# Transposed probabilities leave PSUM through VectorE instead of ScalarE, in a latent-attention transformer layer on eight cores

## The chip, the cores and the metric

The kernel runs on the 8 cores of one Trainium2 chip, one batch element per core, with the same program on each. No core talks to another. The metric is the device time in microseconds of the slowest core. In the text, PE is TensorE, DVE is VectorE, ACT is ScalarE, POOL is GpSimd and SP is the queue engine SyncE.

## The reference

The layer takes x of shape 8 x 2048 x 2048 (batch, tokens, features) in float32. It is attention with a latent bottleneck, then a gated feed-forward block, each with a residual and a layer norm behind it.

```python
q = rmsnorm(x @ q_a_w.T, q_a_ln_w) @ q_b_w.T          # 16 heads, 128 + 64 each
ckv_full = x @ kv_a_w.T                               # 512 latent + 64 rotary
kv = rmsnorm(ckv_full[..., :512], kv_a_ln_w) @ kv_b_w.T
k_nope, v = kv[..., :128], kv[..., 128:]              # per head
# rotary on q_pe and on the one k_pe that all heads share
scores = einsum('bhqd,bhkd->bhqk', query, key_s) * SCALE
probs  = softmax(where(causal, scores, -inf))
attn   = einsum('bhqk,bhkd->bhqd', probs, v)
x = layernorm(x + attn @ o_w.T)
x = layernorm(x + ffn(x))     # silu(g) * u, ternary weights with scales, 5632 wide
```

## The kernel before

The program writes the instruction stream of each engine by hand. `P.op` puts one instruction at the end of an engine's list and can increment a semaphore; `P.w` and `P.wf` put a wait there. Each engine works its list in order, so the order of the calls is the order of the work. The semaphores that matter here are `sAct` (counts ACT's results), `vE` and `vStat` (DVE's results), `tTR` (transposes done by PE) and `tMM` (other matmuls).

The stages follow each other with a barrier between (`gate`): projections of x, the queries, the attention heads (line 589 on), the output projection with the first layer norm, and the feed-forward block.

The attention stage loops over 16 heads. For each head PE forms the keys `kfm` and the values `vtm` out of the latent `c_fm`, and ACT copies them out of PSUM (lines 648 and 666). Then a loop runs over `qc`, the 16 chunks of 128 queries, with two more turns to drain it. A chunk `qc` sees (qc+1)*128 keys, in groups of up to 512 columns, so it has one group for chunks 0 to 3 and four groups for chunks 12 to 15. The scores of a group go to one of five 512-column regions of PSUM (`ring`: four in `pS`, one in `pX`). One turn `qc` does this, in the order of the code:

- For each group PE multiplies queries by keys (line 692), adds the causal mask to the last group (699) and adds the rotary part (703). DVE takes the row maximum of the group (710).
- For the chunk two turns back, `pqc` = qc-2, PE transposes the probabilities in blocks of four tiles of 128 (line 745). The transpose is a matmul of `Ebuf` with `Dg`, a diagonal matrix with the reciprocals of the row sums. The result in `pPT` (two buffers) is copied to `PTsb` (two buffers, line 752). `emit_pv` multiplies the values by it into `pO` (729), one block behind the transposes. ACT copies `pO` to `OX` (763).
- DVE forms the negated maximum over the groups (769). ACT takes the exponential of each group with it as bias, and the row sums with it (778, two instructions each: the activation and the reading of the accumulator).
- DVE adds up the row sums (785), takes the reciprocal (789) and forms `Dg` (793).

Chunk `pqc` has `nkt` = pqc+1 tiles, so its copies are one to four blocks, the last of one to four tiles. There are 40 copies a head, 640 in all. A region of the ring is free again when the exps of its group are done. `pts_free` makes a copy wait until `PTsb` has been multiplied, and `ppt_free` makes the transposes wait until `pPT` has been copied. The same list, under the name `pw_free`, guards these two PSUM buffers where the next head forms its keys.

## Time and profile before

| What | us |
|---|---|
| Median of 2 runs | 5739.92 |
| Lowest and highest of them | 5714.51, 5765.32 |
| The profiled execution, its own time | 5654.77 |
| Its span on the slowest core (core 1) | 5653.3 |
| Spans of the eight cores | 5617.7 to 5653.3 |

The span runs from the first to the last instruction of one core; the execution's own time is 1.5 us longer than it. Rows of the profile give an engine, a line of the kernel, what is written from what, and how long. A busy PE is not PE at its peak, since matmuls overlap. "Idle before" names what ended an engine's wait. Over the whole span PE is busy for 68%, DVE for 33%, ACT for 29%, POOL for 6%.

### The profile page before, as it was taken

How to read it: one execution, taken by the hardware profiler on the slowest of the kernel's cores; microseconds unless marked ns; L12 is line 12 of the kernel's file. 1: busy time of each engine (PE TensorE's matmuls, PEld its weight loads, DVE VectorE, ACT ScalarE, POOL GpSimd, SP SyncE). 2: the span in 40 equal slices, each digit the busy share in tenths (PEclk: the TensorE clock that was granted, in tenths of full speed). 3: DMA queues.
4: the chain of work that ended last, by engine and by line, in shares of the span. 5: the costliest groups of instructions: out<-in, count | busy, mean ns of one | idle time of the engine just before them, and what ended most of it. 6: DMA issues, size and time to landing. Idle time of an engine off the chain costs nothing.

```text
span 5653.3 us, 67407 instructions; the slowest of 8 cores (5617.7 to 5653.3 us)
## 1 busy us (share of the span) xinstructions
PE 3870.8 (68%) x20400; PEld 1847.0 (33%) x20400; DVE 1866.8 (33%) x3822; ACT 1635.9 (29%) x3420; POOL 331.7 (6%) x581
## 2 busy tenths in 40 slices
PE   0456556656666666666355669885998599859986
PEld 0222222223333333333122223342444244424443
DVE  2222322444333333333223233323332233223323
ACT  0000000006565656565100013322332233223322
POOL 0000000000000000000000001111111111101110
PEclk9877778888877878887577779998999899989998
DMA  4111012100000000000311049875887589758975
GB/s 128 44 30 30 27 42 60 30 26 5 9 5 9 5 10 5 9 7 3 103 62 38 30 122 265 272 241 186 282 280 250 190 276 278 243 191 276 283 250 172
DMA packets 209874, 674.49 MB, mean 119 GB/s; under 512 B 30272, under 2 KB 30784, under 8 KB 205440
## 3 DMA queue, kind: packets, MB, share of 16 engines
q1 hardware_dynamic: 130608, 359.51, 20.8%
q0 software_dynamic: 78928, 310.68, 17.1%
q8 instruction: 187, 3.06, 0.2%
q14 instruction: 151, 1.24, 0.1%
HBM read 653.05 MB, written 16.78 MB: 118 GB/s over the span
## 4 chain that ended last, share of the span: by engine, by line
PE 34%; DMA 31%; DVE 13%; issue 11%; ACT 9%; DVEq 1%; SPq 0%; ACTq 0%; POOL 0%; POOLq 0%
DMA stg_gp<-up_l 19%; PE pD L1068 6%; DMA stg_gp<-down_c 5%; PE pPT L526 5%; PE pOP L864 4%; ACT Ebuf L778 4%; PE pQA L362 3%; PE pO L729 3%; ACT PTsb L752 2%; DVE ubf L229 2%; DMA stage<-ow_l 2%; PE pPT L745 2%; DVE stats L710 2%; PE pS L692 2%; PE pPT L641 1%
## 5 line engine op out<-in xcount | busy, mean ns | idle before, releaser
L997 PE MATMUL pU<-OX,ubf 128*128 128x512 bf16 x2816 | 648.6, 384 | 127.3 <-DVE ubf L229 126.4
L988 PE MATMUL pG<-OX,gbf 128*128 128x512 bf16 x2816 | 644.1, 382 | 128.6 <-ACT gbf L226 128.6
L1068 PE MATMUL pD<-h_fm,dbf 128*128 128x512 bf16 x2816 | 636.2, 382 | 84.5 <-DVE dbf L229 80.1
L229 DVE CAST ubf<-stg_gp 128x1024 bf16<-128x1024 f32 x352 | 244.6, 695 | 868.0 <-DMA stg_gp<-up_l 849.3
L729 PE MATMUL pO<-PTsb,vtm 128*128 128x128 bf16 x2176 | 251.3, 248 | 311.8 <-ACT PTsb L752 308.5
L997 PEld LDWEIGHTS pU<-OX,ubf 128*128 128x128 bf16 x2816 | 270.5, 99 | 493.1 <-issue 195.5
L988 PEld LDWEIGHTS pG<-OX,gbf 128*128 128x128 bf16 x2816 | 276.9, 98 | 466.8 <-issue 140.1
L1068 PEld LDWEIGHTS pD<-h_fm,dbf 128*128 128x128 bf16 x2816 | 272.8, 98 | 426.4 <-issue 127.3
L1010 ACT ACTIVATE sig<-pG,gates_sb 128x512 bf16<-128x512 f32 x176 | 120.9, 687 | 872.0 <-DVE tmid L1015 612.7
L226 ACT CAST gbf<-stg_sy 128x1024 bf16<-128x1024 f32 x352 | 351.3, 1040 | 70.8 <-DMA stg_sy<-gate_l 70.5
L752 ACT CAST PTsb<-pPT 128x512 bf16<-128x512 f32 (+3 forms) x640 | 312.6, 524 | 201.3 <-PE pPT L745 200.5
L526 PE MATMUL pPT<-rmsqa_fm,qbw_bf 128*128 128x512 bf16 x1152 | 277.4, 403 | 135.4 <-DVE qbw_bf L191 135.3
L864 PE MATMUL pOP<-ow_bf,OX 128*128 128x512 bf16 x1024 | 278.0, 439 | 109.5 <-DVE ow_bf L191 106.9
L778 ACT ACTIVATE Ebuf<-pS,stats 128x512 bf16<-128x512 f32 (+3 forms) x512 | 314.3, 621 | 88.9 <-DVE stats L769 87.8
L710 DVE TENSOR_REDUCE stats<-pS 128x1 f32<-128x512 f32 (+3 forms) x512 | 289.6, 599 | 122.6 <-PE pS L703 122.0
L226 ACT CAST dbf<-stg_sy 128x1024 bf16<-128x1024 f32 (+1 forms) x192 | 174.3, 971 | 538.0 <-PE pD L1068 538.0
L229 DVE CAST dbf<-stg_gp 128x1024 bf16<-128x1024 f32 (+1 forms) x192 | 122.5, 649 | 546.5 <-DMA stg_gp<-down_c 285.0
L729 PEld LDWEIGHTS pO<-PTsb,vtm 128*128 128x128 bf16 x2176 | 156.8, 108 | 389.8 <-issue 387.9
L221 POOL DMA_DIRECT2D stg_gp<-up_l x352 | 207.4, 589 | 1225.1 <-DVE ubf L229 1113.7
L745 PE MATMUL pPT<-Dg,Ebuf 128*128 128x128 bf16 x2176 | 254.7, 255 | 26.5 <-DVE stats L710 23.5
L692 PE MATMUL pS<-kfm,Q_all 128*128 128x512 bf16 (+3 forms) x512 | 215.2, 420 | 69.1 <-ACT Ebuf L778 42.7
L362 PE MATMUL pQA<-qa_w_bf,x0fm_t 128*128 128x512 bf16 x768 | 235.8, 421 | 20.9 <-DVE x0fm_t L345 20.9
(132 smaller groups left out, 3745.6 us busy)
## 6 DMA issues: line engine op xcount, KB each, us to landing
stg_gp<-up_l POOLq DMA_DIRECT2D x352, 512.0 KB, 6.2
stg_sy<-gate_l SPq DMA_DIRECT2D x352, 512.0 KB, 6.4
stg_sy<-down_c SPq DMA_DIRECT2D x128, 512.0 KB, 5.6
stg_gp<-down_c POOLq DMA_DIRECT2D x128, 512.0 KB, 5.2
stg_sy<-down_c SPq DMA_DIRECT2D x64, 384.0 KB, 6.2
stg_gp<-down_c POOLq DMA_DIRECT2D x64, 384.0 KB, 4.4
stage<-x SPq DMA_DIRECT2D x64, 256.0 KB, 3.2
stage<-ow_l SPq DMA_DIRECT2D x64, 256.0 KB, 3.3
```

What stands on the lines that cost most here:

```text
L226: e.copy(d[:, a:a + cc], tiles[i][:, 0:cc]), inc=cP)
L229: e.tensor_copy(d[:, a:a + cc], tiles[i][:, 0:cc]), inc=cP)
L362: P.op("tensor", lambda e, i=i, d=d, j=j, st=st, sp=sp: e.matmul(pQA[:, j * 512:(j + 1) * 512], x0fm_t[i][:, d * 128:(d + 1) * 128], qa_w_ ...
L526: P.op("tensor", lambda e, pb=pb, sk=slots[k], k=k, cc=cc, piece=piece: e.matmul(pW[pb][:], qbw_bf[:, sk * 512 + cc * 128:sk * 512 + (cc + ...
L710: P.op("vector", lambda e, g=g, n=n, rt=rt, off=off, par=par: e.reduce_max(stats[:, par + g:par + g + 1], rt[:, off:off + n], axis=AX), in ...
L729: P.op("tensor", lambda e, kt=kt, bb=bb, sl=sl, nkt=nkt: e.matmul(pO[:, 0:128], vtm[:, kt * 128:(kt + 1) * 128], PTsb[sl][:, bb * 128:(bb ...
L752: P.op("scalar", lambda e, bn=bn, sl=sl: e.copy(PTsb[sl][:, 0:bn * 128], pPT[sl][:, 0:bn * 128]), inc=sAct)
L778: P.op("scalar", lambda e, ei=ei, g=g, n=n, rt=rt, off=off, par=par: e.activation(Ebuf[ei][:, g * 512:g * 512 + n], rt[:, off:off + n], AF ...
L864: P.op("tensor", lambda e, hv=hv, t=t, j=j, st=st, sp=sp: e.matmul(pOP[:, j * 512:(j + 1) * 512], OX[:, hv * S + t * 128:hv * S + (t + 1) ...
L988: P.op("tensor", lambda e, wi=wi, d=d, gc0=gc0: e.matmul(pG[wi][:], gbf[wi][:, d * 128:(d + 1) * 128], OX[:, d * S + gc0:d * S + gc0 + 512 ...
L997: P.op("tensor", lambda e, wi=wi, d=d, gc0=gc0: e.matmul(pU[wi][:], ubf[wi][:, d * 128:(d + 1) * 128], OX[:, d * S + gc0:d * S + gc0 + 512 ...
L1068: P.op("tensor", lambda e, di=di, hh=hh, jj=jj, ii=ii: e.matmul(pD[di][:], dbf[hh][:, jj * 128:(jj + 1) * 128], h_fm[:, ii * 512:(ii + 1) ...
```

## The change

The copy of the transposed probabilities out of PSUM is taken from ACT and given to DVE. The waits that go with it follow: the copy's own waits stand in DVE's list, it increments `vE` instead of `sAct`, and both PE's product with `PTsb` and the next use of `pPT` wait on `vE`.

```diff
                             def emit_pv(sl, b0, bn, ev):
                                 nonlocal first_pv
-                                P.w("tensor", sAct, ev)
+                                P.w("tensor", vE, ev)
...
-                                P.w("scalar", tTR, tTR.n)
-                                P.wf("scalar", pts_free[sl])
-                                P.op("scalar", lambda e, bn=bn, sl=sl: e.copy(
-                                    PTsb[sl][:, 0:bn * 128], pPT[sl][:, 0:bn * 128]), inc=sAct)
-                                ppt_free[sl] = (sAct, sAct.n)
+                                P.w("vector", tTR, tTR.n)
+                                P.wf("vector", pts_free[sl])
+                                P.op("vector", lambda e, bn=bn, sl=sl: e.tensor_copy(
+                                    PTsb[sl][:, 0:bn * 128], pPT[sl][:, 0:bn * 128]), inc=vE)
+                                ppt_free[sl] = (vE, vE.n)
                                 if pvq is not None:
                                     emit_pv(*pvq)
-                                pvq = (sl, b0, bn, sAct.n)
+                                pvq = (sl, b0, bn, vE.n)
```

DVE's list at the end of a head, before the change. The first rows are the maxima of chunk 15 (L710) and its negated maximum (L769), then the sum, the reciprocal and Dg of chunk 15, and the cast of the next head's weights:

```order
L710 TENSOR_REDUCE stats<-pS 128x1 x3
L710 TENSOR_REDUCE stats<-pX 128x1
L769 TENSOR_REDUCE stats<-stats 128x1
L785 TENSOR_REDUCE stats<-stats 128x1
L789 RECIPROCAL stats<-stats 128x1
L793 TENSOR_SCALAR Dg<-cI,stats 128x128
L191 CAST kvw_bf<-stage 128x512 x2
```

The same place after the change:

```order
L710 TENSOR_REDUCE stats<-pS 128x1 x3
L710 TENSOR_REDUCE stats<-pX 128x1
L752 CAST PTsb<-pPT 128x512 x3
L752 CAST PTsb<-pPT 128x256
L769 TENSOR_REDUCE stats<-stats 128x1
L785 TENSOR_REDUCE stats<-stats 128x1
L789 RECIPROCAL stats<-stats 128x1
L793 TENSOR_SCALAR Dg<-cI,stats 128x128
L752 CAST PTsb<-pPT 128x512 x3
L752 CAST PTsb<-pPT 128x384
L752 CAST PTsb<-pPT 128x512 x4
L191 CAST kvw_bf<-stage 128x512 x2
```

The copies of chunk 13 (14 tiles) stand between the maxima of chunk 15 and its negated maximum; those of chunks 14 and 15 stand behind Dg and ahead of the cast of the weights.

ACT's list at the same place before the change, with the copies of chunk 13, the output copy (L763), the exps of chunk 15 (L778) and the copies of chunks 14 and 15:

```order
L752 CAST PTsb<-pPT 128x512 x3
L752 CAST PTsb<-pPT 128x256
L763 CAST OX<-pO 128x128
L778 ACTIVATE Ebuf,stats<-pS,stats 128x512 x3
L778 ACTIVATE Ebuf,stats<-pX,stats 128x512
L752 CAST PTsb<-pPT 128x512 x3
L752 CAST PTsb<-pPT 128x384
L763 CAST OX<-pO 128x128
L752 CAST PTsb<-pPT 128x512 x4
L763 CAST OX<-pO 128x128
L648 CAST kfm<-pPT 128x512 x4
```

And after it:

```order
L763 CAST OX<-pO 128x128
L778 ACTIVATE Ebuf,stats<-pS,stats 128x512 x3
L778 ACTIVATE Ebuf,stats<-pX,stats 128x512
L763 CAST OX<-pO 128x128 x2
L648 CAST kfm<-pPT 128x512 x4
```

Every PTsb row is gone from ACT's list, and what is left there keeps its order. The lists of PE, POOL and SP have the same rows as before.

## Rows read from the trace of the kernel before

**Rows 1.** The attention stage in the view by stage: us, busy time of each engine.

```profile
1237.00:2737.00 1500.00, 999.19 (x7199) 554.76 (x7197) 545.03 (x1715) 880.14 (x2497) 1.74 (x3) 0.80 0.03 8
```

**Rows 2.** Timeline of one head: first and last negated maximum, last output copy.

```profile
2465.11 0.15 DVE L769 TENSOR_REDUCE stats<-stats 128x1 f32<-128x1 f32 x1
...
2529.66 0.16 DVE L769 TENSOR_REDUCE stats<-stats 128x1 f32<-128x4 f32 x1
...
2541.52 0.27 ACT L763 CAST OX<-pO 128x128 bf16<-128x128 f32 x1 [0.62 <-PE pO L729]
```

**Rows 3.** Timeline (start, duration, engine), one turn, chunk 13 to 14 of a head.

```profile
2427.11 0.69 ACT L778 ACTIVATE Ebuf<-pS,stats 128x512 bf16<-128x512 f32 x1
...
2427.77 0.49 ACT L778 ACTIVATE Ebuf<-pS,stats 128x256 bf16<-128x256 f32 x1
...
2428.45 0.16 DVE L785 TENSOR_REDUCE stats<-stats 128x1 f32<-128x4 f32 x1 [3.20 <-ACT Ebuf L778]
...
2428.55 0.72 PE L745 MATMUL pPT<-Dg,Ebuf 128*128 128x128 bf16 x8
...
2429.08 1.07 ACT L752 CAST PTsb<-pPT 128x512 bf16<-128x512 f32 x2 [0.73 <-PE pPT L745]
2429.22 1.28 DVE L710 TENSOR_REDUCE stats<-pS 128x1 f32<-128x512 f32 x2
...
2430.02 0.38 PE L729 MATMUL pO<-PTsb,vtm 128*128 128x128 bf16 x4 [0.75 <-ACT PTsb L752]
...
2431.01 0.55 DVE L710 TENSOR_REDUCE stats<-pS 128x1 f32<-128x384 f32 x1
...
2431.67 0.16 DVE L769 TENSOR_REDUCE stats<-stats 128x1 f32<-128x4 f32 x1
2432.14 0.27 ACT L763 CAST OX<-pO 128x128 bf16<-128x128 f32 x1 [0.51 <-PE pO L729]
...
2432.31 0.69 ACT L778 ACTIVATE Ebuf<-pS,stats 128x512 bf16<-128x512 f32 x1
```

**Rows 4.** Groups by line and form: busy us, mean ns of one, idle before.

```profile
L752 ACT CAST PTsb<-pPT 128x512 bf16<-128x512 f32 (+3 forms) x640 | 312.6, 524 | 201.3 <-PE pPT L745 200.5
...
L752 ACT CAST PTsb<-pPT 128x512 bf16<-128x512 f32 x448 | 249.1, 589 | 165.4 <-PE pPT L745 164.9
L345 DVE CAST x0fm_t<-pTR 128x512 bf16<-128x512 f32 x64 | 44.3, 692 | 57.8 <-PE pTR L339 57.8
L710 DVE TENSOR_REDUCE stats<-pS 128x1 f32<-128x512 f32 x352 | 228.3, 683 | 0.4 <-issue 0.4
L710 DVE TENSOR_REDUCE stats<-pS 128x1 f32<-128x128 f32 x48 | 13.7, 285 | 122.0 <-PE pS L703 122.0
```

**Rows 5.** Who waited for whom in the attention stage: us in total, times, longest.

```profile
DVE stats L785 <- ACT Ebuf L778: 498.3, 255, 3.9
...
PE pO L729 <- ACT PTsb L752: 308.5, 368, 3.2
```

**Rows 6.** Timeline of the output projection: a DVE copy from PSUM and PE behind it.

```profile
3013.41 0.69 DVE L846 CAST OX<-pTR 128x512 bf16<-128x512 f32 x1 [0.84 <-PE pTR L839]
3014.25 0.58 PE L839 MATMUL pTR<-cI,x1tm 128*128 128x128 bf16 x4 [0.94 <-DVE OX L846]
```

**Rows 7.** Two stretches of a head by stage (granted clock behind POOL), and transposes in the first's clock.

```profile
2484.00:2488.00 4.00, 3.13 (x19) 1.73 (x17) 1.93 (x6) 2.45 (x7) 0.00 (x0) 0.50 0.02 4
...
2505.00:2510.00 5.00, 3.60 (x28) 1.73 (x28) 2.31 (x7) 3.64 (x10) 0.00 (x0) 1.00 0.02 3
...
2476.03 0.63 PE L745 MATMUL pPT<-Dg,Ebuf 128*128 128x128 bf16 x4
```

**Rows 8.** Timeline at the end of a head, after the exps of chunk 15.

```profile
2532.80 1.09 ACT L752 CAST PTsb<-pPT 128x512 bf16<-128x512 f32 x2
...
2533.63 0.26 DVE L793 TENSOR_SCALAR Dg<-cI,stats 128x128 bf16<-128x128 bf16 x1 [0.18 <-DVE stats L789]
2533.76 0.58 PE L729 MATMUL pO<-PTsb,vtm 128*128 128x128 bf16 x4 [3.09 <-ACT PTsb L752]
```

## Prediction

> **What bounds the kernel now.** I read the stages first, then the attention stage instruction by instruction. The stage view gives the attention stage 1500 us of the 5653.3 us span, with PE busy for 999, ACT for 880 and DVE for 545 us of it [rows 1]. No engine is full, so a chain of waits sets the time there. The groups that the change moves are ACT's 640 copies of PTsb, 312.6 us in all: 448 are of 512 columns, 0.589 us each [rows 4], all in this stage. The waits of the stage look like an invitation to move them: DVE stands idle for 498.3 us behind ACT's exps, and PE waits 308.5 us for these copies [rows 5].
>
> One turn of the loop over query chunks shows who waits for whom; rows 3 are the turn from chunk 13 to chunk 14 of one head. ACT's exps of 512 columns start 0.66 us apart (2427.11 to 2427.77). When the last has ended, DVE sums (2428.45), takes the reciprocal, scales Dg and starts the maxes of the next chunk at 2429.22: 1.00 us after the last exp's own slot of 0.45 us (2427.77 + 0.45 = 2428.22). The four maxes start 0.60 us apart. The negated max stands at 2431.67, and exps can follow it by 0.25 us. Beside this, and on ACT, which is idle then, the copies of chunk 12 start at 2429.08, before the first max. PE multiplies with them from 2430.02, the output copy of OX comes at 2432.14 and the next exps at 2432.31.
>
> So before, the loop is exps, sum and Dg, maxes, negated max, exps, and the copies lie beside the maxes. I test that with a sum over one head, whose negated maxes run from 2465.11 (chunk 0) to 2529.66 (chunk 15), 64.55 us [rows 2]. Chunk q has q/4 (rounded down) full groups of 512 columns and one ragged group. That makes 21 full groups of exps (chunks 0 to 14) by 0.665 us = 14.0, 15 ragged ones by about 0.50 = 7.5, 24 full groups of maxes (chunks 1 to 15) by 0.60 = 14.4, 15 ragged by 0.41 = 6.2, and 15 stretches of 1.00 from exps to maxes = 15.0. The ragged values are means that I estimate between the rows at 512 and those at fewer columns. That is 57.1 us; with 0.43 us from the end of the last max's slot to the exps in each turn (15 by 0.43 = 6.5) it makes 63.6, against 64.55 measured. The copies thus cost at most about 1 us a head now.
>
> **The change part by part.** Every copy of PTsb goes from ACT to DVE, 640 of them; the waits of PE on them change only the semaphore. The text of PE, POOL and SP is the same. What matters is the place on DVE: behind all maxes of chunk q, ahead of the negated max of chunk q, the copies of chunk q-2 stand now. DVE works in order, so three things follow.
>
> First, the duration. A copy of this form on DVE takes 0.692 us (the same form, TensorE's output to a 16-bit tile) against 0.589 on ACT [rows 4], and PE follows it 0.84 us after its start (3013.41 to 3014.25) [rows 6]. Alone that is 0.10 us for each copy on the path.
>
> Second, the place. The copies can start only behind the last max: one slot after its start, at about 2431.5 in rows 3 (2431.01 and some 0.46 for 384 columns) instead of 2429.08, 2.4 us later. The 0.43 us at the end of the loop is replaced by a chain C: copy, product, OX copy, exps. With PE at 2.4 GHz four 128-column matmuls take 0.38 us and 0.21 of PE's time; at 1.2 GHz 0.63 and 0.43 [rows 3, 7]. From a matmul's end to OX 0.10, from OX to the exps 0.17.
> One block of four tiles: 0.84 + 0.38 + 0.26 = 1.48 us (1.73 at 1.2 GHz).
> Two blocks: the second copy starts 0.60 later: 2.08 (2.33).
> Three: the third transposes use the first's buffer, so they follow the first copy and the first product: 0.84 + 0.21 + 0.38 + 0.12 until the third copy, 0.84 for it, 0.38 + 0.26 behind it: 3.03 (0.84 + 0.43 + 0.63 + 0.12 + 0.84 + 0.63 + 0.26 = 3.75).
> Four: the fourth copy 0.60 behind the third: 3.63; at 1.2 GHz its transposes are the later ones, and it is 4.61.
> Each tile that the last block lacks takes off 0.13 for the copy (maxes of 128 and 512 columns take 0.285 and 0.683 [rows 4], and the copy at 512 takes the same as a max) and 0.05 (0.11) for each PE group of the last block on the path: one with up to two blocks and with four, two with three blocks (and with four at 1.2 GHz).
>
> Now the turns of a head. Chunks 2 to 5 copy one block, 6 to 9 two, 10 to 13 three, 14 and 15 four, and within each class the last block has 1, 2, 3, 4 tiles. The clock is 1.2 GHz (0.50) in the early turns and 2.4 (1.00) later, rising behind chunk 7 [rows 7]. The sums of C are then 5.5 + 7.3 + 10.7 + 6.3, and 0.43 for chunk 1, which copies nothing: 30.2 us. With 1.2 GHz throughout they are 5.5 + 7.9 + 12.9 + 7.6 + 0.43 = 34.3. The body of a head becomes 57.1 + 30.2 = 87.3 us (91.4), against 64.55: 22.8 us more (26.9).
>
> Third, the end of the head. The copies of chunk 14 start at 2532.80 now, straight behind ACT's exps. On DVE they come behind Dg of chunk 15, which starts at 2533.63 and is followed 0.17 later: 1.0 us later. PE already waits for them there, 3.09 us [rows 8]. These and the copies of chunk 15 form a chain with some eight links, each 0.10 us longer. Together 1.8 us. The cast of the next head's weights falls behind these copies too; it takes 0.43 us and lies beside the last product, so I count nothing (without that cover, at most 0.4 us a head, 7 in all).
>
> What is unloaded from ACT buys nothing: exps wait for OX's copy, which needs the last product, and that needs the last copy. The later stages are untouched.
>
> Sum: 22.8 + 1.8 = 24.6 us a head at the present clock, by 16 heads 394 us; with PE at 1.2 GHz throughout, 28.7 by 16 = 459 us. The turns grow by a third with the same matmuls in them, so PE is less busy, and I expect the higher clock to be lost in a part of the turns: I take the middle, 425 us. The profiled execution took 5654.77 us (its span is 5653.3), which makes 6080 us. It was 1.5% below the median of the runs shown, 5739.92, and the result will be such a median, so the forecast is 5740 + 425 = 6165, say 6160 us.
>
> DVE's pace is weighed against one page. The maxes in rows 3 start 0.60 us apart though each lasts 0.68. The Trainium skill, VectorE: DVE Perf Modes, section "The DRAIN you can't avoid", says that the next operation does not start until the pipe is empty. By that rule each further copy in a row would cost 0.08 us more, some 25 of them a head, 2 us, or 30 us in all; by the row nothing. The trace disagrees with the rule for maxes, and I go by the row.
>
> **The rivals.** *The clock stays at 1.2 GHz.* Worked out above: 459 us, 5740 + 459 = 6199. For it: PE's share of busy time falls in every turn. Against it: in the late turns the clock stays at 1.00 although PE already waits in every turn.
>
> *The copies find a hole in DVE.* If the maxes of a chunk were done before its predecessor's transposes, a copy would start when it does now, and only the 0.10 us for each link would be left: about 27 links a head by 0.10 by 16 = 43 us, 5783, no measurable difference. DVE's idle 498.3 us speaks for it; but that idle time lies ahead of the sum at 2428.45, while the copies are wanted at 2429.08, when the maxes begin. It would need maxes that start at least 2.4 us earlier.
>
> *ACT is what the loop waits for* (the other sign). If the exps stood ready and only the copies kept ACT from them, the move would free them. The place is the copies ahead of each group of exps: 312.6 us of ACT's 880. At the end of a head the copies of chunk 14 do stand behind the exps for about 2.5 us. If a quarter of those 312 us were on the path, the time would fall by 78 us to 5662. It decides in favour where the negated max is ready long before the exps start; in rows 3 it is 0.64 us earlier, and OX's copy, not PTsb's, is what comes last. The Trainium skill, TensorEngine Tiling (Array Packing), section "PSUM Bottleneck", advises to use both ScalarE and VectorE for emptying PSUM, which is this rival's rule. By it the step gains; the rows above say that DVE is in the loop exactly when it would be needed.
>
> **How the numbers follow.** My forecast (the clock lost in part) has a chance of 0.60, the clock lost throughout 0.33, the hole in DVE 0.04, ACT as the bound 0.03. The first two are both slower. A measurement of this kernel can tell about 2%, 115 us, from no change. So slower by over 2% has 0.93, within 2% 0.05 (the hole, and a small gain of the third), faster 0.02. The range: at its low end 5655 + 394 = 6049 if the new runs are like the profiled one; at its high end the slower of the runs shown, 5765, with 459 = 6224; the sum for 64.55 us fell short by 1 us a head, and the rule on DVE gives 30 us, so I allow about 45 us above and 30 below: 6020 to 6270.
>
> **What would show it right or wrong.** The attention stage grows from 1500 to about 1925 us, the other stages keep their times. PTsb's copies on DVE take 0.69 us at 512 columns. In a late turn the first copy starts one slot (0.2 to 0.6 us) behind the last max's start, and PE's wait for the copies grows from 308.5 us by several hundred. A turn with four groups takes 9.1 to 10 us instead of 6.6, one with a single group about 1 us more. ACT's busy time falls by some 310 us and its idle time grows by over 700. The granted clock of the stage falls below 0.80. I am wrong if the copies start before the maxes end, if the negated max comes later than OX's copy, or if the late turns stay under 8 us.

## The result and the profile after

The changed kernel takes 6129.99 us in the median of 11 runs, against 5742.74 us of the kernel before in the runs beside it. The ratio is 1.0776 with a 95% interval of 1.0706 to 1.0846: slower by 7.8%. (It leaves out executions in which some cores ran some per cent slower at a lower clock, whatever the kernel; both medians contain such, so they differ by less, 387 us or 6.7%.) The median lies inside the range of the forecast and 30 us below its value. The profiled execution took 6138.3 us.

The head of the profile page, PE's line and the line of the copies, of the kernel after:

```profile
span 6136.8 us, 67407 instructions; the slowest of 8 cores (6069.4 to 6136.8 us)
...
PE 4075.5 (66%) x20400; PEld 1952.4 (32%) x20400; DVE 2194.7 (36%) x4462; ACT 1318.8 (21%) x2780; POOL 328.2 (5%) x581
...
L752 DVE CAST PTsb<-pPT 128x512 bf16<-128x512 f32 (+3 forms) x640 | 368.6, 604 | 126.1 <-PE pPT L745 124.8
```

The attention stage of the kernel after, in the view by stage (us, busy time of PE, PE's weight loads, DVE, ACT and POOL, granted clock); it answers to [rows 1]:

```profile
1301.00:3259.00 1958.00, 1148.27 (x7187) 644.83 (x7185) 868.89 (x2349) 564.28 (x1857) 1.74 (x3) 0.66 0.02 7
```

The stage grew from 1500 to 1958 us. ACT's busy time fell by 316 us, DVE's rose by 324, and the granted clock fell from 0.80 to 0.66. I compare this stage between kernels by the time from the first to the last output copy (L763): 1274.9 to 2725.9 before, 1338.0 to 3248.1 after, 1451 against 1910 us, so 459 us more. Over the eight cores of the same executions it is 1445 to 1457 and 1910 to 1917 us. The whole span differs by 483.5. The rest lies in stages that the change does not touch: the first output copy came 63 us later in this one execution, while it stands between 1273 and 1289 in every run of the experiments, and the stages behind attention were 39 us shorter.

Who waits for whom in that stage of the kernel after, us in total, times, longest; it answers to [rows 5]:

```profile
ACT OX L763 <- PE pO L729: 1210.0, 256, 7.4
...
PE pO L729 <- DVE PTsb L752: 677.1, 398, 4.4
DVE stats L785 <- ACT Ebuf L778: 642.1, 256, 3.9
```

PE's wait for the copies has doubled, from 308.5 to 677.1 us, and ACT waits 1210 us for the products. DVE, now the engine with more work, waits more for the exps than before (642 against 498 us). No engine became full: a chain got longer. The turn from chunk 13 to chunk 14 of one head, timeline of the kernel after; it answers to [rows 3]:

```profile
2855.85 0.69 ACT L778 ACTIVATE Ebuf<-pS,stats 128x512 bf16<-128x512 f32 x1
...
2857.85 0.49 ACT L778 ACTIVATE Ebuf<-pS,stats 128x256 bf16<-128x256 f32 x1
...
2858.53 0.16 DVE L785 TENSOR_REDUCE stats<-stats 128x1 f32<-128x4 f32 x1 [3.60 <-ACT Ebuf L778]
...
2859.18 1.06 PE L745 MATMUL pPT<-Dg,Ebuf 128*128 128x128 bf16 x8
2859.30 1.28 DVE L710 TENSOR_REDUCE stats<-pS 128x1 f32<-128x512 f32 x2
...
2861.09 0.55 DVE L710 TENSOR_REDUCE stats<-pS 128x1 f32<-128x384 f32 x1
2861.56 1.28 DVE L752 CAST PTsb<-pPT 128x512 bf16<-128x512 f32 x2
2862.60 0.58 PE L729 MATMUL pO<-PTsb,vtm 128*128 128x128 bf16 x4 [2.35 <-DVE PTsb L752]
...
2864.59 0.15 DVE L769 TENSOR_REDUCE stats<-stats 128x1 f32<-128x4 f32 x1
...
2865.41 0.27 ACT L763 CAST OX<-pO 128x128 bf16<-128x128 f32 x1 [6.98 <-PE pO L729]
2865.57 0.69 ACT L778 ACTIVATE Ebuf<-pS,stats 128x512 bf16<-128x512 f32 x1
```

Exps to exps is 9.72 us. PE has begun the transposes at 2859.18, but the copy starts at 2861.56, right behind the last max. From there it is 4.01 us to the next exps. The negated max (2864.59) is ready 0.98 us before them.

The end of the same head: the copies of chunk 14 (2879.29) now follow Dg of chunk 15, and PE waits 4.04 us for them, where it was 3.09 [rows 8].

```profile
2879.12 0.26 DVE L793 TENSOR_SCALAR Dg<-cI,stats 128x128 bf16<-128x128 bf16 x1 [0.18 <-DVE stats L789]
2879.29 1.29 DVE L752 CAST PTsb<-pPT 128x512 bf16<-128x512 f32 x2
2880.34 0.58 PE L729 MATMUL pO<-PTsb,vtm 128*128 128x128 bf16 x4 [4.04 <-DVE PTsb L752]
```

### The profile page after: what moved, and what is told of

It is laid out like the page before. It is cut to its first block, busy times and chain, and to the rows that moved or that the text cites. A ratio compares the mean times of both kernels' runs of the same rounds, so it can differ in the third digit from the quotient of the medians.

```text
span 6136.8 us, 67407 instructions; the slowest of 8 cores (6069.4 to 6136.8 us)
## 1 busy us (share of the span) xinstructions
PE 4075.5 (66%) x20400; PEld 1952.4 (32%) x20400; DVE 2194.7 (36%) x4462; ACT 1318.8 (21%) x2780; POOL 328.2 (5%) x581
## 4 chain that ended last, share of the span: by engine, by line
PE 36%; DMA 28%; DVE 17%; issue 12%; ACT 5%; DVEq 1%; SPq 0%; POOL 0%; ACTq 0%; POOLq 0%
DMA stg_gp<-up_l 17%; PE pD L1068 5%; PE pPT L526 5%; DMA stg_gp<-down_c 5%; PE pOP L864 4%; PE pO L729 4%; PE pQA L362 4%; DVE PTsb L752 4%; DVE stats L710 3%; ACT Ebuf L778 3%; PE pPT L745 2%; PE pS L692 2%; DVE ubf L229 2%; PE pS L703 2%; DMA stage<-ow_l 2%
## 5 line engine op out<-in xcount | busy, mean ns | idle before, releaser
L729 PE MATMUL pO<-PTsb,vtm 128*128 128x128 bf16 x2176 | 294.9, 280 | 677.8 <-DVE PTsb L752 677.1
L729 PEld LDWEIGHTS pO<-PTsb,vtm 128*128 128x128 bf16 x2176 | 183.4, 121 | 767.7 <-issue 764.8
L752 DVE CAST PTsb<-pPT 128x512 bf16<-128x512 f32 (+3 forms) x640 | 368.6, 604 | 126.1 <-PE pPT L745 124.8
L526 PE MATMUL pPT<-rmsqa_fm,qbw_bf 128*128 128x512 bf16 x1152 | 295.7, 422 | 135.0 <-DVE qbw_bf L191 134.8
L710 DVE TENSOR_REDUCE stats<-pS 128x1 f32<-128x512 f32 (+3 forms) x512 | 289.6, 599 | 122.5 <-PE pS L703 122.5
L763 ACT CAST OX<-pO 128x128 bf16<-128x128 f32 x256 | 67.8, 265 | 1210.0 <-PE pO L729 1210.0
L778 ACT ACTIVATE Ebuf<-pS,stats 128x512 bf16<-128x512 f32 (+3 forms) x512 | 315.3, 625 | 40.5 <-DVE stats L769 39.6
L745 PE MATMUL pPT<-Dg,Ebuf 128*128 128x128 bf16 x2176 | 289.0, 287 | 25.3 <-DVE stats L710 25.2
L692 PE MATMUL pS<-kfm,Q_all 128*128 128x512 bf16 (+3 forms) x512 | 265.7, 519 | 23.5 <-ACT Ebuf L778 8.8
L362 PE MATMUL pQA<-qa_w_bf,x0fm_t 128*128 128x512 bf16 x768 | 263.0, 461 | 20.8 <-DVE x0fm_t L345 20.8
```

The lines of the kernel that those rows point to most:

```text
L362: P.op("tensor", lambda e, i=i, d=d, j=j, st=st, sp=sp: e.matmul(pQA[:, j * 512:(j + 1) * 512], x0fm_t[i][:, d * 128:(d + 1) * 128], qa_w_ ...
L526: P.op("tensor", lambda e, pb=pb, sk=slots[k], k=k, cc=cc, piece=piece: e.matmul(pW[pb][:], qbw_bf[:, sk * 512 + cc * 128:sk * 512 + (cc + ...
L710: P.op("vector", lambda e, g=g, n=n, rt=rt, off=off, par=par: e.reduce_max(stats[:, par + g:par + g + 1], rt[:, off:off + n], axis=AX), in ...
L729: P.op("tensor", lambda e, kt=kt, bb=bb, sl=sl, nkt=nkt: e.matmul(pO[:, 0:128], vtm[:, kt * 128:(kt + 1) * 128], PTsb[sl][:, bb * 128:(bb ...
L752: P.op("vector", lambda e, bn=bn, sl=sl: e.tensor_copy(PTsb[sl][:, 0:bn * 128], pPT[sl][:, 0:bn * 128]), inc=vE)
L778: P.op("scalar", lambda e, ei=ei, g=g, n=n, rt=rt, off=off, par=par: e.activation(Ebuf[ei][:, g * 512:g * 512 + n], rt[:, off:off + n], AF ...
```

## The experiments

The stage is the time between the first and the last output copy on the slowest core of one profiled execution; over the eight cores of one execution it spreads by 1 to 17 us, so differences of that size say nothing. The clock is that of the stage. Runs are the lowest and the second lowest time (of e3 the lowest alone); where a ratio to the kernel before (same chip) has an interval, it is given.

| Kernel | copies on | stage, us | clock | runs, us | ratio |
|---|---|---|---|---|---|
| before | ACT | 1451 | 0.80 | 5647, 5656 | 1 |
| changed | DVE | 1910 | 0.66 | 6101, 6104 | 1.0776 (1.0706 to 1.0846) |
| e1 late sums | DVE | 1640 | 0.73 | 5840, 5867 | |
| e2 late sums | ACT | 1414 | 0.80 | 5605, 5609 | |
| e3 negated max first | DVE | 2008 | 0.65 | 6202 | |
| e4 copies twice | ACT | 1802 | 0.67 | 6012, 6014 | |
| e5 filler matmuls | DVE | 1845 | 0.77 | 6008, 6013 | 1.0628 (1.0570 to 1.0686) |
| e6 alternate | both | 1627 | 0.73 | 5809, 5816 | 1.0270 (1.0234 to 1.0306) |
| e7 late sums, max last | DVE | 1527 | 0.79 | 5707, 5721 | 1.0105 (1.0067 to 1.0143) |
| e8 late sums, split, late out | both | 1361 | 0.80 | 5540, 5541 | 0.9782 (0.9745 to 0.9818) |
| e9 late sums, late out | ACT | 1340 | 0.81 | 5549, 5571 | 0.9814 (0.9744 to 0.9885) |
| e10 late sums, late out | DVE | 1512 | 0.76 | 5694, 5703 | |
| e11 maxes between copies | DVE | 1737 | 0.66 | 5930, 5946 | 1.0495 (1.0448 to 1.0541) |
| e12 copy's wait last | DVE | 1852 | 0.68 | 6052, 6061 | |

**e1: sums and Dg one turn later, behind the copies.** The statements of L784 to L795 (sum, reciprocal, Dg, and the entry in `pendq`) become a function `late_stats` that is called one turn later, behind the copies, and in the first draining turn ahead of them. The negated max goes ahead of the copies.

```diff
+                        if qc < TC:
+                            P.w("vector", vStat, vStat.n)
+                            P.op("vector", lambda e, ngr=ngr, par=par: e.reduce_max(
+                                stats[:, par + 4:par + 5], stats[:, par:par + ngr],
+                                axis=AX, negate=True), inc=vStat)
+                            neg_done = vStat.n
-                        if len(pendq) >= 2 or (qc >= TC and pendq):
+                        if pendq and pendq[0][0] <= qc - 2:
...
                             po_free = (sAct, sAct.n)
+                        if late is not None:
+                            late()
+                            late = None
...
                             exp_done = sAct.n
+                            late = late_stats
```

> The changed kernel (copies on DVE), with DVE's sum, reciprocal and Dg of chunk q-1 put behind the maxes, the negated max and the copies of turn q, where they stood ahead of the maxes of turn q. DVE then need not wait for the exps before it takes the next maxes. Theory A (the copies are dear because DVE stands in the loop exps, sum, Dg, maxes, copies, product, exps): most of the loss comes back, 20 to 31 us a head, 320 to 490 us in all, so 5640 to 5810 us. Rival B (the copy itself is dear on DVE, by its duration or by contention): the 640 copies are all still there, so the time stays within 50 us of 6130. Rival C (the clock is what costs): it comes back only as far as the granted clock of the attention stage rises from 0.66.

Measured: 5840 and 5867 us, stage 1640. The same 640 copies on the same engine, 270 us less in the stage. Rival B falls, since nothing about the copies is different. Rival C is not settled by this run, since the granted clock rose too, from 0.66 to 0.73; e11 and the table of the parts of a head, in the section on the prediction, settle it. Theory A expected 320 us at least and so was too high: the rest is looked for in e3 and e7.

**e2: the same on the kernel before.** The same edit with the copies on ACT.

> The same move of sum, reciprocal and Dg, and the negated max ahead of the copies in program order, in the kernel before (copies on ACT). Theory A: the loop loses its stretch from exps to maxes; where one or two groups are in a turn 0.7 to 1.4 us a turn are gained, at four groups 0.1 to 0.5, since the copies and products are as long there; 0 to 12 us a head by whether the clock holds, so 5550 to 5740 us. Rival B says nothing of this kernel: no change, 5740 us. If the gain is above 2%, this version beats both kernels.

Measured: 5605 and 5609 us, stage 1414, 37 us less than before. This is inside the expected span but low, and the place is not what I wrote. The median spacing of output copies over the 16 heads shortens only between chunks 6 and 10 (4.27 to 3.65, 5.35 to 4.36, 5.58 to 4.71, 5.93 to 5.42 us), while for the chunks copied in one block, where I expected 0.7 us a turn or more, it is the same as before (2.76, 3.18, 3.61). So in the kernel before DVE's loop was not alone in setting the turn: a second chain of nearly equal length, scores, transposes, copy on ACT, product, OX, stood beside it. The waits of ACT in the attention stage of the kernel before had shown it:

```profile
ACT OX L763 <- PE pO L729: 179.8, 256, 1.0
ACT Ebuf L778 <- DVE stats L769: 92.0, 129, 2.0
```

ACT waited for the product in all 256 turns, and after the output copy it still waited for the negated max in 129 of them. So the negated max came last in about half of the turns, and the output copy in the others.

**e3: the negated max ahead of the copies.** In the changed kernel; the statements of L768 to L772 are moved up to the start of the block of `pqc`.

> The changed kernel with the negated max ahead of the copies on DVE. Theory A: exps wait for the output copy OX, never for the negated max, so nothing is gained; the small instruction waits for the last max's write and delays the first copy by about 0.3 us, 14 turns by 16 heads by 0.3 = 67 us slower than the changed kernel, 6200 us. Rival D (exps wait for the negated max behind the copies): up to 0.6 us a turn and block come back, 100 us or more faster, below 6030 us.

Measured: 6202 us, stage 2008, 98 us more than the changed kernel. Rival D falls: the exps do not wait for the negated max. The price of the small instruction is 98 / (14 x 16) = 0.44 us a turn, above the 0.3 expected; 0.36 of it is the start of the first copy, 0.83 us behind that of the last max where it was 0.47 (copies of chunk 12). The lesson runs both ways: whatever stands ahead of the first copy on DVE is paid in full.

**e4: each copy twice on ACT,** in the kernel before. It does work that the reference does not need.

```diff
                                     PTsb[sl][:, 0:bn * 128], pPT[sl][:, 0:bn * 128]), inc=sAct)
+                                P.w("scalar", sAct, sAct.n)
+                                P.op("scalar", lambda e, bn=bn, sl=sl: e.copy(
+                                    PTsb[sl][:, 0:bn * 128], pPT[sl][:, 0:bn * 128]), inc=sAct)
```

> The kernel before with each copy of PTsb done twice on ACT, the second behind the first. Theory A: ACT has room, and only the copies on PE's path in turns with three and four groups and at the end of a head cost; 6 to 11 us a head, 100 to 180 us, 5840 to 5920 us. Rival E (ACT is what the loop waits for, so that the change should have gained): all 640 second copies count, 313 us or more, above 6050 us.

Measured: 6012 us, stage 1802, 351 us more than before. My estimate of 100 to 180 was wrong by a factor of two, and the size is that which rival E named (313 or more), though the time stayed under its 6050. The timeline of e4 shows a turn with one block (L752 the first, L755 the second copy, L766 the output copy):

```profile
2652.54 0.59 ACT L752 CAST PTsb<-pPT 128x512 bf16<-128x512 f32 x1 [0.69 <-PE pPT L745]
...
2653.21 0.59 ACT L755 CAST PTsb<-pPT 128x512 bf16<-128x512 f32 x1
2653.84 0.15 DVE L772 TENSOR_REDUCE stats<-stats 128x1 f32<-128x2 f32 x1
2654.15 0.58 PE L729 MATMUL pO<-PTsb,vtm 128*128 128x128 bf16 x4 [1.76 <-ACT PTsb L755]
...
2654.83 0.27 ACT L766 CAST OX<-pO 128x128 bf16<-128x128 f32 x1 [1.03 <-PE pO L729]
2654.99 0.69 ACT L781 ACTIVATE Ebuf<-pS,stats 128x512 bf16<-128x512 f32 x1
```

The second copy adds 0.67 us, and the negated max is ready 1.15 us before the exps. The spacings of output copies grow in every turn, from 0.47 us with one block (2.76 to 3.23) to 2.61 with four (6.43 to 9.04). The second chain of e2 thus had little slack in the kernel before: about 0.2 us with one block, 0.1 with four. That is a chain and not a full engine: ACT is busy for 1197 us of the 1803, and e9 below gives ACT all copies with no measurable loss. The granted clock fell here too, to 0.67, with no copy on DVE, so a part of the 351 us, not measured alone, is the slower matmuls.

**e5: filler matmuls in PE's wait,** in the changed kernel. To place them, the two other waits of the first product went ahead of the copy's wait.

```diff
-                                P.w("tensor", vE, ev)
                                 if first_pv:
                                     P.w("tensor", sAct, kv_ready)
                                     P.wf("tensor", po_free)
                                     first_pv = False
+                                    if qc < TC:
+                                        for _ in range(3 * (qc // 4)):
+                                            P.op("tensor", lambda e: e.matmul(
+                                                pO[:, 256:512], cI[:], kfm[:, 0:256],
+                                                start=True, stop=True))
+                                P.w("tensor", vE, ev)
```

> The changed kernel with 3, 6 or 9 extra matmuls of 256 columns (chunks 4 to 7, 8 to 11, 12 to 15) that PE does in each turn where it waits for the first copy; their result lies in unused columns of pO and is never read. They are work that the reference has not. Theory A with the clock as its second part: the fillers cost nothing where PE waits (9 take 1.9 us at 1.2 GHz, the wait is 2.4), the granted clock of the attention stage rises from 0.66 to 0.75 or more, and the transposes and products on the path get shorter: 2 to 4 us a head, 30 to 70 us faster than the changed kernel's fast runs (6101 to 6138), so near 6060. Rival F (the clock has no part in the loss): no change, or slower by the fillers.

Measured: 6008 us, stage 1845, clock 0.77. It looked like 65 us for the clock. But the turns of chunks 2 and 3, which have no fillers, were 0.2 us shorter as well. The two moved waits were the other half of the edit, and e12 takes them alone.

**e12: the copy's wait last, no fillers.**

> The changed kernel with one thing of e5 alone: before the first product of a turn PE waits first for the values and for pO, and last for the copy (in the changed kernel the copy's wait stands first and the two others behind it). In e5's trace PE's product starts 0.83 us after the first copy, in the changed kernel 1.04, also in turns without filler matmuls. Theory W (two further wait instructions behind the released one cost 0.2 us a turn, and they gave e5 its gain): 256 turns by 0.21 = 54 us off the changed kernel's attention stage of 1910, so 1850 to 1860, with the granted clock at about 0.66; the rest of e5 (1845) is then 5 to 15 us for the clock less the fillers. Theory C (the clock gave e5 its 65 us): the stage stays near 1910.

Measured: 6052 us, stage 1852, 58 us less than the changed kernel at a clock of 0.68. Theory W holds. The same turn (copies of chunk 2), first in the changed kernel, then in e12:

```profile
2794.01 0.55 DVE L752 CAST PTsb<-pPT 128x384 bf16<-128x384 f32 x1
...
2794.92 0.48 PE L729 MATMUL pO<-PTsb,vtm 128*128 128x128 bf16 x3 [1.89 <-DVE PTsb L752]
```

```profile
2696.09 0.55 DVE L752 CAST PTsb<-pPT 128x384 bf16<-128x384 f32 x1
...
2696.79 0.48 PE L729 MATMUL pO<-PTsb,vtm 128*128 128x128 bf16 x3 [1.68 <-DVE PTsb L752]
```

The product follows the copy's start by 0.91 us in one and 0.70 in the other. What is left for the fillers and the clock in e5 is 1852 - 1845 = 7 us (over the eight cores 1852 to 1862 against 1844 or 1845). The way from the first copy to the exps is 1.4 us a head shorter in e5 than in e12, 22 us in all, and the end of a head with the start of the next one 1.1 us longer, 17 us. No run raised the clock and changed nothing else: e5 adds work to PE, and e7 below moves the sums.

**e6: every second block on DVE,** the others on ACT.

```diff
-                                P.w("tensor", vE, ev)
+                                P.wf("tensor", ev)
...
+                                if (b0 // 4) % 2:
                                     P.w("vector", tTR, tTR.n)
...
                                     ppt_free[sl] = (vE, vE.n)
+                                else:
+                                    P.w("scalar", tTR, tTR.n)
...
+                                    ppt_free[sl] = (sAct, sAct.n)
-                                pvq = (sl, b0, bn, vE.n)
+                                pvq = (sl, b0, bn, ppt_free[sl])
```

> The changed kernel with only every second block of a chunk (the 2nd and 4th) copied on DVE, the 1st and 3rd on ACT again. Rival G (both engines should empty PSUM, so a split beats either): faster than the kernel before. Theory A: turns with one block are as before; with two or more the copy on DVE waits for the maxes all the same, so a turn of two blocks costs 0.6 to 1 us and one of three or four 1.1 to 2 us more than before: 12 to 15 us a head, 195 to 245 us slower than before on the same chip, about half of the change's loss.

Measured: ratio 1.0270, stage 1627, 176 us more than before (195 to 245 expected). The spacings with one block are as before (2.76, 3.18, 3.61). Rival G falls for this order of DVE's list: 256 of the 640 copies on DVE (16 of the 40 of a head) cost 176 of the 459 us.

**e7: as e1, with the negated max behind the copies again.**

> As e1_after_late_sums (copies on DVE, sums and Dg one turn later), but with the negated max behind the copies, as in the changed kernel. Theory A: it takes its 0.3 us off the way to the first copy; 14 turns by 16 heads by 0.3 = 67 us, up to 80, faster than e1 (5840 to 5867), so 5770 to 5800. If exps now wait for the negated max behind the copies, it is slower than e1.

Measured: ratio 1.0105, 5707 us, stage 1527: 113 us less than e1 (67 to 80 expected). All 640 copies are on DVE and the loss is down from 459 to 76 us of the stage. The turn from chunk 13 to 14 in e7's timeline (L786 exps, L711 maxes, L756 copies, L767 output copy):

```profile
2496.71 0.69 ACT L786 ACTIVATE Ebuf<-pS,stats 128x512 bf16<-128x512 f32 x1
...
2497.52 0.69 DVE L711 TENSOR_REDUCE stats<-pS 128x1 f32<-128x512 f32 x1 [0.88 <-PE pS L704]
...
2498.71 0.49 ACT L786 ACTIVATE Ebuf<-pS,stats 128x256 bf16<-128x256 f32 x1
...
2500.22 0.55 DVE L711 TENSOR_REDUCE stats<-pS 128x1 f32<-128x384 f32 x1
2500.68 1.28 DVE L756 CAST PTsb<-pPT 128x512 bf16<-128x512 f32 x2
...
2503.99 0.27 ACT L767 CAST OX<-pO 128x128 bf16<-128x128 f32 x1 [4.70 <-PE pO L733]
...
2504.15 0.69 ACT L786 ACTIVATE Ebuf<-pS,stats 128x512 bf16<-128x512 f32 x1
```

The first max starts 0.81 us behind the exps' start, beside them, where in the changed kernel it was 3.45 us behind it. The turn takes 7.44 us instead of 9.72, with the same instructions. Of the 2.28 us, 1.74 lie ahead of the first copy and 0.54 behind it.

**e8: late sums, blocks on both engines, output copy behind the exps.** e1's edit, e6's, and the copy to OX moved behind the exps of its turn in ACT's list.

```diff
-                            P.w("scalar", tMM, o_mm)
-                            P.op("scalar", lambda e, h=h, pqc=pqc: e.copy(
-                                OX[:, h * S + pqc * 128:h * S + (pqc + 1) * 128],
-                                pO[:, 0:128]), inc=sAct)
-                            po_free = (sAct, sAct.n)
+                            ox_todo = (pqc, o_mm)
...
                             late = late_stats
+                        if ox_todo is not None:
+                            xqc, x_mm = ox_todo
+                            ox_todo = None
+                            P.w("scalar", tMM, x_mm)
+                            P.op("scalar", lambda e, h=h, xqc=xqc: e.copy(
+                                OX[:, h * S + xqc * 128:h * S + (xqc + 1) * 128],
+                                pO[:, 0:128]), inc=sAct)
+                            po_free = (sAct, sAct.n)
```

> Late sums, negated max ahead of the copies, the 2nd and 4th block on DVE and the 1st and 3rd on ACT, and the output copy to OX behind the exps of its turn instead of ahead of them. Theory A: DVE is out of the loop by the late sums, and the exps need no longer wait for the last product; by the same working as for the prediction a head takes 60 to 74 us instead of 76, so 0 to 240 us less than the kernel before: 5450 to 5650, best guess 5530. If it is under e2_before_late_sums (5605 to 5669), copies on DVE pay once DVE is out of the loop.

Measured: ratio 0.9782, 5540 us, as expected. It beats both kernels.

**e9: e8 with all copies on ACT.**

> The kernel before (all copies on ACT) with late sums and with the output copy to OX behind the exps; against e8 only the 2nd and 4th blocks change their engine. Theory A: with both orders mended a copy on ACT is on no worse a place than one on DVE and 0.1 us shorter, so this is as fast as e8 or up to 2 us a head faster: 5500 to 5560 us, ratio to before 0.97 to 0.98. Rival G (splitting the copies over both engines is what made e8 fast): slower than e8 by the copies that ACT then does more, towards e2, 5600 us or above.

Measured: ratio 0.9814 with an interval that covers e8's. The stage is 1340 us against 1361. The orders of the sums and of the output copy make the gain, and the split of the copies adds nothing that can be measured.

**e10: e8 with all copies on DVE,** negated max behind them.

> All copies on DVE, late sums, negated max behind the copies, output copy behind the exps. ACT has only exps and OX then. Theory A: DVE carries maxes, copies and sums, 4 to 6 us in a late turn, and is close to the bound, but the exps lie beside it: a head of 67 to 79 us by the same working, so between 5% below and 1% above e7 (5707 to 5738), best guess 5620; slower than e8 by some 80 us. If the copies on ACT were in the way of exps (rival E), this is the fastest of all, below 5540.

Measured: 5694 us, stage 1512. It is slower than e8 by 154 us (80 expected) and about as fast as e7 (1527). With the copies on DVE the late output copy brings 15 us, hardly more than the spread over the cores; with them on ACT it brought 1414 - 1340 = 74. Against e9, which has the late sums and the late output copy too, the copies on DVE cost 1512 - 1340 = 172 us. Rival E falls: ACT is nearly free here and the kernel is not faster.

**e11: the maxes between the copies.** On DVE the list becomes copy, max, copy, max, and so on; the sums stay where they were.

```diff
+                                def one_max(g=g, n=n, rt=rt, off=off, par=par, mm=gmm[g]):
-                                P.w("vector", tMM, gmm[g])
+                                    P.w("vector", tMM, mm)
...
+                                maxq.append(one_max)
...
                                 ppt_free[sl] = (vE, vE.n)
+                                if maxq:
+                                    maxq.pop(0)()
...
+                        while maxq:
+                            maxq.pop(0)()
                         if qc < TC:
                             P.w("vector", vStat, vStat.n)
```

> The changed kernel with DVE's maxes of chunk q between the copies of chunk q-2 (copy, max, copy, max, ...; what is left of the maxes behind), sums where they were. The same work on DVE, only the place of the copies is another. Theory A: the first copy no longer waits for all maxes; PE's products lie beside the later maxes, and the loop is exps, sums, maxes and copies: 0.5 to 1 us a turn less than the changed kernel, 8 to 10 us a head, 120 to 160 us, so 5950 to 6000 against 6101 to 6138. Rival B (the copy on DVE is dear by itself, not by its place): no change.

Measured: ratio 1.0495, 5930 us, stage 1737, 173 us less than the changed kernel (120 to 160 expected), at the same clock of 0.66. DVE's part of the timeline in the turn from chunk 14 to chunk 15 (L755 copies, L712 maxes, L776 negated max, L800 Dg):

```profile
2679.91 0.26 DVE L800 TENSOR_SCALAR Dg<-cI,stats 128x128 bf16<-128x128 bf16 x1 [0.18 <-DVE stats L796]
2680.68 0.69 DVE L755 CAST PTsb<-pPT 128x512 bf16<-128x512 f32 x1 [0.51 <-PE pPT L748]
2681.29 0.68 DVE L712 TENSOR_REDUCE stats<-pS 128x1 f32<-128x512 f32 x1
...
2684.61 0.68 DVE L712 TENSOR_REDUCE stats<-pX 128x1 f32<-128x512 f32 x1
2685.39 0.16 DVE L776 TENSOR_REDUCE stats<-stats 128x1 f32<-128x4 f32 x1
```

The first copy waits for PE's transposes alone. DVE does the same work, and only the place of the copies is another. That shows the place as a cost by itself, without a change of the clock.

## Why the prediction was right

The order of DVE's list was named as the cost, and the runs bear it out: with the maxes put between the copies the stage is 173 us shorter at the same clock (e11), with the maxes freed from the sums 383 (e7), and both keep every copy on DVE. The signs that were named came too: turns with four groups of keys take 8.5 to 10.1 us (medians over the heads; 9.1 to 10 were forecast), those with a single group 0.7 to 1.0 us more than before.

That the forecast of 6160 us and the median lie only 30 us apart is in part luck. The forecast adds 425 us to a median of 5740. The medians differ by 387 us, less than either of its two sums, and the ratio of 1.0776 means about 440 us (an estimate from it). In the stage the loss is 459 us, the sum for the rival that the clock is lost throughout, but it is made up in another way, as the steps show:

*The duration.* The 448 copies of 512 columns were priced at 0.692 us and take 0.684 (294.5 us in all). 640 copies take 368.6 us, 56 more than on ACT. About 27 of the 40 copies of a head lie on the chain; by 0.10 and 16 that is 43 us, a tenth of the loss. In the late turns the first product follows the start of the first copy by 0.94 us with the copy on ACT and 1.04 on DVE. No run changed the duration alone; that share is by the working.

*The place.* The turn in the trace follows the working up to the first copy: 1.00 us from the last exp's slot (2857.85 + 0.45) to the first max at 2859.30, and the copy one slot behind the last max's start (2861.09 to 2861.56).

*C, the way from the first copy to the exps, was too small.* By its own rule the prediction has 3.56 us for this turn with the matmuls at 1.2 GHz (4.61 less 3 x 0.35 for three missing tiles); the trace has 4.01. Of the missing 0.45, 0.20 is in one place. I took PE to start 0.84 us behind the copy, from a row of another stage [rows 6]; at the first product of a turn it is 1.04 (2861.56 to 2862.60). Rows 3 had shown it: there PE follows ACT's first copy by 0.94 us though the copy lasts 0.59. e12 shows its cause, two more wait instructions behind the one that is released, and its price, 58 us of the changed kernel's stage. The kernel before has the same two waits, and no run took them away there: it is a term that the forecast sized too small and not one that the change brought. The other 0.25 lies behind the third copy, from which the trace needs 1.79 us (2863.78 to 2865.57) and the rule for missing tiles left 1.54. (Redone by their rules, the prediction's sums of C are 30.4 and 34.2 instead of 30.2 and 34.3, which is 4 us more and 2 us less in all.)

*The clock.* I took it as partly lost: 394 us with it, 459 without, and the middle, 425. The granted clock did fall in the late turns (0.62 to 0.68 where it was 0.98 to 1.00), and the stage lost 459 us. But the clock was lost in part, as forecast, and not throughout, and it carries only a part of the 65 us between the two sums. The stretch from the first copy to the output copy, in the turn shown above of the changed kernel and in the same turn of e7, by stage (granted clock behind POOL):

```profile
2861.56:2865.41 3.85, 2.33 (x19) 1.90 (x20) 2.23 (x6) 0.00 (x1) 0.00 (x0) 0.50 0.00 0
```

```profile
2500.68:2503.99 3.31, 1.53 (x18) 1.09 (x18) 2.46 (x8) 0.01 (x1) 0.00 (x0) 1.00 0.00 0
```

The same copies and products take 0.54 us less at 1.00 (2.4 GHz) than at 0.50 (1.2 GHz); the prediction's rules give 0.47 for this turn (3.56 less 3.09). So where the clock was lost, it cost about what the working has. C is the way from the start of a turn's first copy to the start of its exps. Read from the timelines and summed over a head (mean of the 16 heads, us):

| Kernel | exps of chunk 0 to exps of chunk 15, without C | C, sum of 14 turns |
|---|---|---|
| the prediction, clock as before | 57.5 | 29.8 |
| the prediction, clock lost | 57.5 | 33.9 |
| changed | 57.5 | 35.3 |
| e12 copy's wait last | 57.6 | 32.7 |
| e5 filler matmuls | 57.5 | 31.3 |
| e3 negated max first | 62.7 | 35.9 |
| e1 late sums | 41.5 | 33.9 |
| e7 late sums, max last | 35.4 | 33.4 |
| e11 maxes between copies | 39.8 | 42.7 |

(57.5 is the 57.1 of the working with the 0.43 of chunk 1.) The part ahead of the copies came as forecast. What e1 and e7 gave back, 17 and 24 us a head, lies there but for 1.4 and 1.9 us, so it is the order of the list and not the clock that gave it back. C is 5.5 us a head longer than with the clock as before. Of this 2.6 us are the two waits (e12), and 1.4 (e5 against e12) to 1.9 us (e7 against the changed kernel, stage clock 0.79 and 0.66) go with the clock, 22 to 30 us in all; about 1 us is the rest of the sizes. Against it, the head that the prediction took (64.55 us) is 1.2 us shorter than the mean head before (65.8), and the end of a head costs 1.6 us in the mean, not 1.8: 24.6 + 5.5 - 1.2 - 0.2 = 28.7 us a head, by 16 the 459 us. So the forecast's own choice, 31 us for the clock on top of 394, came out about right, and what carried the stage past its 425 us are the waits. The granted clock by stage for the late turns of one head, kernel after, then kernel before:

```profile
2822.00:2846.00 24.00, 14.55 (x88) 8.12 (x88) 12.72 (x33) 6.53 (x21) 0.00 (x0) 0.68 0.00 1
2846.00:2874.00 28.00, 17.96 (x102) 9.43 (x102) 14.06 (x33) 8.21 (x27) 0.00 (x0) 0.62 0.00 1
```

```profile
2488.00:2510.00 22.00, 14.46 (x121) 8.01 (x118) 11.45 (x34) 15.15 (x42) 0.00 (x0) 0.98 0.00 1
2510.00:2530.00 20.00, 13.41 (x109) 6.79 (x110) 9.55 (x27) 13.69 (x40) 0.00 (x0) 1.00 0.01 2
```

*The end of a head.* From the last negated max to the last output copy it is 13.95 us (2874.73 to 2888.68) against 11.86: 2.1 us more in this head, 1.8 predicted.

*What was wrong in the reading of before.* "The copies thus cost at most about 1 us a head now" does not hold. The sum of DVE's loop came within 1 us of the measured head, but a second chain was as long beside it. e4 showed it by lengthening that chain (351 us), e2 by shortening the first (37 us only), e9 by shortening both (111 us). The forecast did not suffer, since both chains run through the copies once they are on DVE. A forecast for e4 or e2 from that sentence alone did.

*The two rules.* The Trainium skill, VectorE: DVE Perf Modes, section "The DRAIN you can't avoid", says that the next DVE operation does not start until the pipe is empty, and also that one which is not held starts earlier. The rows of the changed kernel agree with the second sentence and not with the first: the maxes start 0.60 us apart at 0.68 us of duration, and the first copy starts 0.47 us behind a max of 0.55 us. The advice of the Trainium skill, TensorEngine Tiling (Array Packing), section "PSUM Bottleneck", to use both engines for PSUM was tried as such: in the old order the split costs 2.7% (e6), in the new order it is worth no more than all copies on ACT (e8, e9).

*The rivals.* The hole in DVE was not there: the first copy starts behind the last max in every turn. ACT as the bound is refused by e10, where ACT has neither the copies nor an output copy ahead of the exps and the kernel is slower than e9 by over 120 us.

## What to carry to other kernels

Before an instruction is moved to an idle engine, find what that engine does at the moment at which the instruction is wanted, since idle time elsewhere in the turn does not help; here DVE was idle during the exps and busy right behind them. When a sum over one chain comes out at the measured time, look for a second chain of the same length before calling anything beside it free. Where the engine's list is in the way, moving small instructions of the list (here three, by one turn) can give back most of what the choice of the engine cost: 383 of 459 us. It does not make the engines equal: with late sums and late output copy the stage is 1340 us with the copies on ACT and 1512 on DVE.

## What the runs showed of the hardware

Two waits in PE's list behind the one that is released last cost 0.2 us although both are long fulfilled: the product starts 0.91 us after the copy's start with them behind, 0.70 with them ahead, and 256 turns made it 58 us. Put the wait that is fulfilled last at the end.

The granted clock of this stage did not hang on which engine copies. It was lower, the longer the stage into which the same matmuls were spread: 0.81 at 1340 us (e9), 0.80 at 1451 (before), 0.79 at 1527 (e7), 0.73 at 1627 and 1640 (e6, e1), 0.67 at 1802 (e4, all copies on ACT), 0.66 at 1910 (changed), 0.65 at 2008 (e3). Three runs stand beside this row: 0.76 at 1512 (e10), 0.66 at 1737 (e11) and, with filler matmuls in PE's waits, 0.77 at 1845 (e5). What causes it was not tested further. Its price was small here, 22 to 30 of the 459 us, since in these turns PE mostly waits.
